# Expert routing of a two-layer mixture kernel: one-hot inversion at the end against lists scattered to DRAM batch by batch

## The reference

```python
x = x + _L0_xattn_ref(ctx_768, _layernorm(x), mask, ...)     # 4 heads; keys: 1024 latents + 77 context rows
x = x + _L0_ffn_ref(_layernorm(x), router_w, w1, b1, w2, b2) # 8 experts, F=1024, relu
x = x + _L1_xattn_ref(_layernorm(x), ctx_768, ...)           # 16 heads, 77 keys
x = x + _L1_ffn_ref(_layernorm(x), gate_w, w1, w2, w3)       # 8 experts, F=512, silu gate
```

```python
logits = x_flat @ router_w.T
probs = softmax(logits); top_w, top_idx = top_k(probs, 2)
top_w = top_w / (sum(top_w) + 1e-9)
out = sum over the two chosen experts of expert(x) * top_w
```

## Time and profile before

| what | value |
|---|---|
| median of 3 runs | 1673.76 us (1672.48 to 1675.39) |
| the profiled execution | 1674.64 us, its span 1672.9 us |
| PE busy | 1475.3 us (88%) |
| DVE busy | 1025.3 us (61%) |
| ACT busy | 837.3 us (50%) |
| POOL busy | 668.4 us (40%) |
| granted TensorE clock, mean | 0.923 of full speed |

### The profile page before, as it was taken

The page is one execution under the profiler, slowest core; times in us unless marked ns, Lnnn a source line. Parts: engine busy times, 40 slices in busy tenths (PEclk is TensorE's granted clock), DMA queues, the critical chain, the costliest instruction groups (busy, mean ns, idle before and its releaser), DMA issues. The chain is left out here.

```text
span 1672.9 us, 36937 instructions
## 1 busy us (share of the span) xinstructions
PE 1475.3 (88%) x12752; PEld 1098.7 (66%) x12752; DVE 1025.3 (61%) x1887; ACT 837.3 (50%) x1583; POOL 668.4 (40%) x495
## 2 busy tenths in 40 slices
PE   6799798898898569999999996999978579999996
PEld 2424334334227559989889984777768469988885
DVE  5666676667667844555554444888858834444543
ACT  2675766766654425556664541667644422222221
POOL 3500402304200015554444443777750036565554
PEclk8899899899895579999999997999985789999998
DMA  5411321313216454567885434100006263355553
GB/s 171 164 51 51 125 75 50 125 50 106 71 51 226 151 213 106 143 163 223 236 233 127 102 65 122 34 25 26 27 1 224 91 205 65 61 138 134 142 133 70
DMA packets 110607, 191.53 MB, mean 114 GB/s; under 512 B 10928, under 2 KB 68580, under 8 KB 110180
## 3 DMA queue, kind: packets, MB, share of 16 engines
q1 hardware_dynamic: 80407, 149.44, 26.6%
q0 software_dynamic: 27264, 37.24, 12.8%
q10 hardware_dynamic: 2791, 2.84, 0.6%
HBM read 122.53 MB, written 66.96 MB: 113 GB/s over the span
## 5 line engine op out<-in xcount | busy, mean ns | idle before, releaser
L1426 PE MATMUL e_ph<-e_zTt,weights_a 128*128 128x256 f16 x2688 | 306.1, 275 | 0.1
L1426 PEld LDWEIGHTS e_ph<-e_zTt,weights_a 128*128 x2688 | 264.9, 99 | 32.7 <-issue 0.4
L1368 POOL DMA_INDIRECT e_zt<-token_parts,slot_token x142 | 146.7, 1033 | 209.7 <-issue 201.7
L1481 ACT ACTIVATE e_h<-e_ph,e_b 128x256 f32<-128x256 f32 (+1 forms) x344 | 128.3, 436 | 154.7 <-PE e_ph L1426 154.3
L1378 POOL DMA_INDIRECT token_rows<-e_ysb,slot_token x71 | 123.2, 1735 | 184.7 <-DVE e_ysb L1554 141.4
L1440 PE MATMUL e_pyt<-weights_b,e_hh 128*128 x1136 | 194.2, 273 | 2.5 <-issue 1.1
L703 ACT ACTIVATE probs<-lower_banks,shift 128x1024 f32<-128x1024 f32 x128 | 137.7, 1112 | 72.9 <-PE lower_banks L577 72.9
L760 DVE TENSOR_TENSOR acc<-acc,probs 128x1024 f32<-128x1024 f32 (+1 forms) x112 | 136.9, 1222 | 52.0 <-ACT probs L703 50.2
L1536 DVE TENSOR_TENSOR e_hl<-e_h,e_hh 128x512 f16<-128x512 f32 x142 | 94.4, 690 | 110.8 <-ACT e_hh L1492 110.6
L1378 POOL DMA_INDIRECT out_dram<-e_ysb,slot_token x71 | 113.1, 1592 | 113.7 <-DVE e_ysb L1557 76.8
L1440 PE MATMUL e_pyt<-weights_b,e_hl 128*128 x568 | 154.8, 273 | 0.0
(11 more groups left out here) (250 smaller groups left out, 2970.8 us busy)
## 6 DMA issues: line engine op xcount, KB each, us to landing
x_sb<-weight_parts SPq DMA_DIRECT2D x30, 1024.0 KB, 7.2
weight_parts<-w_split SPq DMA_DIRECT2D x32, 512.0 KB, 3.3
weights_a<-weight_parts SPq DMA_DIRECT2D x16, 1024.0 KB, 7.4
x_sb<-in_u SPq DMA_DIRECT2D x24, 512.0 KB, 5.3
weight_parts<-x_sb SPq DMA_DIRECT2D x24, 512.0 KB
w_raw<-in_w1T SPq DMA_DIRECT2D x16, 512.0 KB, 4.6
w_raw<-in_w2T SPq DMA_DIRECT2D x16, 512.0 KB, 4.6
weights_b<-weight_parts SPq DMA_DIRECT2D x8, 1024.0 KB, 9.6
```

Of the source, the lines that this page charges most:

```text
L1368: pool.indirect_dma_start(zt[:, i % 2, c, :], None, g.zrows, at).then_inc(ld[i % 2], 16)
L1426: last = pe.matmul(out[:, f, :], weights_up(i, e, wp, k, per[i] * q + f), zTs[:, s, 2 * zp + k, 0:cols[i] * P], start=(n == 0), stop=(n == 5))
L1481: last = act.activation(parted(hidden(h32, n), i)[:, f, :], parted(ph[:, bank_of(i, q)], i)[:, f, :], ACT.Relu, bias=b1[:, bass.ds(e, 1), ...
```

## The change

The one-hot inversion goes. Each expert has a list of CAP = 4096 entries of 8 bytes (token, share) in DRAM. A token's slot is 4096 e + rank, where the rank is counted batch by batch with a running total (`carry`), so the entries of a batch can be written as soon as it is routed: POOL scatters them with one indirect DMA for each tile and choice, 16 for a batch, 64 for a layer. The lists are filled with spare tokens beforehand. When all have landed, ACT loads the entries of the first four tiles (`SOON`) into `slot_tab`, and SP those of the others in `experts`, between its `bring_home` calls; each reads its start from SBUF into a register first. In layer 0, batches 0 to 2 are routed inside steps 4 to 27 of the attention of the following batch (`host`), so `route` has only batch 3 left. AHEAD becomes 3 in layer 0. The loops over batches in `attention0` are written out, and the first half's output moves from step 24 to step 29. The core of the diff:

```diff
+def rank(pe, g, r, b, n, prk):
+    pe.wait_ge(r.tallied, 2 * n - 1)
...
+    pe.matmul(out, g.ones16[:], each(g.carry[:, b:b + 1, :], TB + 1), start=True, stop=False)
+    pe.matmul(out[:, 0:TB, :], g.ones16[:], each(g.base16[:].rearrange("p (o e) -> p o e", o=1), TB), start=False, stop=False)
+    pe.matmul(out[:, 0:TB, :], g.upper16[:], r.wk16[:, t0:t0 + TB, :], start=False, stop=False)
+    for d in range(TB):
+        last = pe.matmul(out[:, d + 1:, :], g.ones16[:], each(r.wk16[:, t0 + d:t0 + d + 1, :], TB - d),
+                         start=False, stop=(d == TB - 1))
...
+def slots(dve, r, b, n, prk):
+    ts = slice(b * TB, (b + 1) * TB)
+    dve.wait_ge(r.rk_done, n)
...
+    step(dve, r, dve.tensor_tensor(r.prod[:], r.oh[:, :, ts, :], ranks, ALU.mult))
+    step(dve, r, dve.tensor_reduce(r.slot[:, :, ts], r.prod[:], AX.X, ALU.add))
+    dve.tensor_copy(r.sloti[:, :, ts], r.slot[:, :, ts]).then_inc(r.slotted, 1)
...
+def scatter(pool, g, r, layer, t):
+    for k in range(2):
+        at = bass.IndirectOffsetOnAxis(ap=r.sloti[:, k, t:t + 1], axis=0)
+        pool.indirect_dma_start(g.lists[layer], at, r.pay[:, t, k, :], None).then_inc(g.scattered[layer], 16)
...
+def bring_table(eng, g, layer, i, tile):
+    n, col, cols = tile
+    s = eng.value_load(g.start[0:1, n:n + 1], min_val=0, max_val=E * CAP)
+    eng.dma_start(g.slot_tab[:, col:col + cols, :].bitcast(I32),
+                  g.lists[layer][bass.ds(s, P * cols), :].rearrange("(p c) w -> p c w", c=cols)
+                  ).then_inc(g.tab_in[layer][tab_group(i)[0]], 16)
```

In `attention0`, on PE, ACT, DVE and POOL (HOST_FROM = 4, HOST_PICK = 21, HOST_RANK = 25; they are called with b - 1, after the step's own work):

```diff
+            def host(b, n):
+                j, odd = divmod(n - HOST_FROM, 2)
+                if not odd and 1 <= j <= TB:
+                    host_logits(b, j - 1)
+                if not odd and 0 <= j < TB:
+                    host_turn(b, j)
+                if n == HOST_RANK:
+                    rank(pe, g, rt, b, b + 1, prkh)
...
+            def host(b, n):
+                j, odd = divmod(n - HOST_FROM, 2)
+                if odd and 0 <= j < TB:
+                    host_copy(b, j)
+                    host_high(b, j)
+                if n == HOST_RANK:
+                    exponents(act, rt, b, b + 1)
...
+            def host(b, n):
+                if n == HOST_PICK:
+                    dve.wait_ge(hlg_done, TB * (b + 1))
+                    read_logits(dve, rt, b, plgh)
+                    pick_top(dve, g, rt, b, b + 1, 0)
...
+                if n == HOST_RANK + 1:
+                    weigh(dve, rt, b, b + 1)
+                if n == HOST_RANK + 2:
+                    slots(dve, rt, b, b + 1, prkh)
...
+                for j in range(TB):
+                    scatter(pool, g, rt, 0, b * TB + j)
```

The end of `route` on ACT, and the start of `experts` on SP and POOL:

```diff
+            act.wait_ge(mapped, 1)
+            act.wait_ge(g.scattered[layer], 32 * T)
+            for i in range(SOON):
+                bring_table(act, g, layer, i, tile_shape(i))
...
-            for e in range(AHEAD, E):
+            upto = SOON
+            for e in range(AHEAD[layer], E):
+                for i in range(upto, min(upto + 2 * TB, NT)):
+                    bring_table(sp, g, layer, i, tile_shape(i))
+                upto = min(upto + 2 * TB, NT)
                 bring_home(sp, g, layer, e)
             if layer == 0:
                 fetch(0)
...
+                group, members = tab_group(i)
+                pool.wait_ge(g.tab_in[layer][group], 16 * members)
```

More of the change, by code:

```diff
@@ L514, in pipeline, with batches @@
                         stage(s - lag)
[L516 to L520, removed]
+        def batches(body):
+            for b in range(B):
+                body(b, b + 1 < B)
         @block.tensor
@@ L883, with tab_group, tile_shape @@
 SINGLES_FROM = 2 * PAIRS - NT
-AHEAD = 5
+CAP = B * S
+TOGETHER = 2
+SOON = 4
+AHEAD = (3, 5)
 AFTER = 2
 LAST = (B - 1) * TB
+def tab_group(i):
+    if i < SOON:
+        return i, 1
+    group = (i - SOON) // TOGETHER
+    return SOON + group, min(TOGETHER, NT - SOON - group * TOGETHER)
+def tile_shape(i):
+    alone = sum(x > SINGLES_FROM and (x - SINGLES_FROM) % 2 == 1 for x in range(i))
+    if i > SINGLES_FROM and (i - SINGLES_FROM) % 2 == 1:
+        return PAIRS + alone, C * PAIRS + alone, 1
+    return i - alone, C * (i - alone), C
 def bring_home(eng, g, layer, e):
@@ L942, in route @@
+        cnti, blocksi, pairsi, oddi = (m.sb(nm(f"ei{i}"), [1, E], I32) for i in range(4))
+        pairs, odd, cum_pairs, cum_odd = (m.sb(nm(f"e{i}"), [1, E]) for i in range(4))
+        ends, leap, apart = (m.sb(nm(f"seg{i}"), [1, SEGMENTS]) for i in range(3))
+        at = m.sb(nm("tile_at"), [1, NT])
+        beyond = m.sb(nm("beyond"), [1, NT, SEGMENTS])
+        begin = m.sb(nm("begin"), [1, NT])
+        owner = m.sb(nm("owner"), [1, NT], I32)
         pz = [m.ps(nm(f"pz{i}"), [P, 4, P]) for i in range(2)]
@@ L976, in _ @@
         def _(pool):
[L977 to L987 removed]
+            number(pool, r)
@@ L988, in _, with turn @@
+            pool.memset(apart[:, E - 1:E], -float((E - 1) * CAP)).then_inc(ready, 1)
+            for b in range(B0, B):
+                pool.wait_ge(r.paid, b - B0 + 1)
+                pool.wait_ge(r.slotted, b - B0 + 1)
+                for t in range(b * TB, (b + 1) * TB):
+                    scatter(pool, g, r, layer, t)
         @block.tensor
         def _(pe):
-            def turn(t):
-                pe.wait_ge(z_done, t + 1)
-                if t >= 2:
-                    pe.wait_ge(ev, t - 1)
+            def turn(l):
+                pe.wait_ge(z_done, l + 1)
+                if l >= 2:
+                    pe.wait_ge(ev, l - 1)
@@ new lines, in _ @@
+            dve.wait_ge(g.stat_roots, RUN - 1)
+            if layer == 0:
+                summarise(dve, g, RUN, EARLY, T, False)
+            for l in range(R):
+                center(l)
+            for l in range(T - FIRST):
+                token_low(l)
+                if l + R < T - FIRST:
+                    dve.wait_ge(lo_done, l + 1)
+                    if FIRST + l + R == EARLY:
+                        dve.wait_ge(g.stat_roots, RUN)
+                    center(l + R)
+                if l == 1 and layer == 1:
+                    summarise(dve, g, RUN, EARLY, T, False)
+                if l >= TB and l % TB == AFTER:
+                    choose(B0 + l // TB - 1)
+                if l >= TB and l % TB == AFTER + 3:
+                    weigh(dve, r, B0 + l // TB - 1, l // TB)
+                    slots(dve, r, B0 + l // TB - 1, l // TB, prk)
```

578 lines of the change are left out of this document (318 added, 260 removed).

## The result

The changed kernel takes 1735.4 us (median of 4 runs, 1731.8 to 1748.4), the kernel before 1674.6 in the same batch: ratio 1.0376, 95% interval 1.0319 to 1.0433. It is slower, by 60.8 us where 39.5 were forecast. The profiled execution took 1731.8 us, with a span of 1730.1, against a span of 1672.9 before.

A forecast was written before the change was run, and what follows sets the result against it. PE was taken to bound attention0, chains of dependent work both routes. Host work +39, route of layer 0 -42.5, experts of layer 0 +22 and route of layer 1 +21 sum to +39.5: 1674.6 becomes 1714 us, range 1660 to 1750.

The forecast's parts named there:

- Host work in attention0: Term: hosted tiles' work on full PE lengthens attention0 by 13 us a batch, three batches, +39 us.
- the sum of 4.64 us: Attention0: loop of PE's step, ACT's copy, cast and exponentials takes 4.64 us for two steps, 4.5 taken, against 3.27.
- Scatters on POOL in attention0: Term: 16 scatters, 20 us, fit a 24 us gap ahead of the next batch's roots, hidden, 4 us to spare.
- Route of layer 0: Term: with only batch 3 left to route, the first gather comes at 556.2 in place of 598.66, -42.5 us.
- Experts of layer 0: Term: SP issues 39 tables and five experts before fetch(0); ACT waits 34.5 us, PE hides 12.5, +22 us, bounds 7.5 and 42.
- Route of layer 1: Term: 64 scatters on POOL move the first gather from 1344.26 to 1365.2, +21 us, bounds +17 and +63.
- POOL is solid with 64 scatters: Sign in layer 1's route: POOL's queue has no gaps, and the first gather comes 109 us after the route's start.
- no stall at tile 2: Rival, experts of layer 0: tables at 0.75 us or less and faster weights keep the fetch hidden; 1692 us, chance 0.20.
- attention absorbs: Rival, attention0: the 4.64 us loop overlaps more than thought and absorbs the host work; 1689 us, chance 0.10.
- cheap scatters: Rival, both routes: POOL's time falls with row size to 0.35 us a scatter; 1660 us, chance 0.15.
- dear ones: Rival, attention0 and both routes: scatters at 1.92 us each, late roots in two batches; 1780 us, chance 0.10.

The follow-up runs named there:

- The cast's move: The changed kernel with the hosted cast to float16 moved from ACT to DVE, after its sum of an odd step: 1728.5 us in one run.
- the tables spread: The changed kernel with fetch(0) and fetch(1) first, then four tables, five bring_homes, and 35 tables two at a time in SP's tile loop: 1703.2 us (1.0156).
- scatters-last run: The changed kernel, but in layer 1's route POOL starts its 64 scatters only when the slots of all four batches are there: 1754.3 us in one run.
- paced run: The changed kernel with a memset of 1024 columns on POOL, waited for, behind every second scatter of layer 1: 1760.6 us in one run.
- ACT's stream shifted: The changed kernel with 24 one-element copies at the start of ACT's part in the route of layer 1: 1737.4 us in one run.

## Why the prediction was right and where not

The direction was right and the time lay in the range, by a sum in which one term was 18 us short, two more were short by 5 and 3.5, and another was 9 us too high. That the last one took back a third of the others is luck; without it the time would have been 1744 us, still inside the range.

*Host work in attention0*, +39 forecast, +30.1 measured. The mechanism held: copies wait for PE's transposes, and two steps with a hosted tile take 4.42 us (212.41 to 216.83) against 4.5 forecast and 3.27 before. Eight of them give 9.2 us, a batch is 10.6 us longer, so the rest (`weight_high` in the loop, last logits, `rank`, late sums) costs 1.4 us by difference and not the 3.2 that I added. The cast's move, worth 0.2 us of its 0.41 for two steps, shows that the loop runs through ACT but not strictly one part after the other, as the sum of 4.64 us had it.

*Scatters on POOL in attention0*, "hidden, with 4 us to spare", held between batches: behind the scatters of the first hosted batch POOL is idle for 4.0 us ahead of the first root (287.93), which waits for DVE. The step that failed is the last batch: behind it no head follows, and the block ends with a wait for the landing. I had named no cover for that end. It costs 3.5 us: the landing ends 0.4 us after the last store, and POOL's drain of 4.0 us stands behind it.

*Route of layer 0*, -42.5 forecast, -41.8 measured; scatters 18.2 us after its start, a cadence of 1.27 us, first gather 47 us after its start. Right in every part, the landing (3.5 us) and the four tables included.

*Experts of layer 0*, +22 forecast, +31.5 measured for the block itself (+26.8 with attention1). The place and the cause were right, and the runs showed both. The term was undersized: a table cost SP 1.18 us (16 in 18.8 us) and not 1.1, ACT's first `weight_high` came 74.4 us after the first gather, 37.0 later than before, and ACT waited 41.0 us, not 34.5; of that PE hid 8 us (41.0 - 33.2), not 12.5. PE's wait stands at tile 4, as forecast, but it ends with DVE's copy of the transposed tokens and not with a bank from ACT: that copy waits in DVE's order behind `e_hl`, and this for ACT (DVE idle for 40.6 us). With the tables spread, 31.7 us come back. A slip of my own in this term: 39 tables at 0.35 us less are 13.7 us, so the lower bound was 8.4 and not 7.5.

*Route of layer 1*, +21 forecast, +39.3 measured, and here the working failed: "POOL is solid with 64 scatters". The first scatter came 22.8 us after the start (20.6 forecast), the cadence was right, and a hole of 15.4 us stood between scatters 32 and 33, which is most of the 18 us. My sum let the tiles of batches 1 to 3 run on beside the scatters as before; the scatters-last run shows them doing so when no scatter runs, and the paced run nearly so at 1.74 us a scatter. Of the path that the sum took, POOL's queue, the price was right; what it lacked is that the scatters delay the work that feeds them.

The rivals: "no stall at tile 2" and "attention absorbs" are refuted by the waits and by the run without hosting; cheap scatters and dear ones both by the median of 0.96 us.

## What to carry to other kernels

When work is moved to a queue, price what stands behind it in that queue customer by customer, and spread cheap, late-needed DMAs between the urgent ones: here the order of 39 small loads on SP cost 32 us, and moving only the first two victims ahead gave back 11. Work put inside a block that ends with a barrier is hidden only if its last completion is early, too, with whatever the engine still runs behind it: here a wait of 0.4 us put a drain of 4.0 us on the path. A gain seen in one execution of one version has to be looked for again in the next: the 7 us of the cast were gone. A producer that streams indirect DMAs beside a fine-grained loop between engines can slow the loop: look for idle stretches whose inputs are ready by the rows.

## What the runs showed of the hardware that was not expected

Back-to-back scatters (128 rows of 8 bytes every 1.27 us) delay the hand-over from PE to ACT. It begins when 8 to 10 of them have been issued and grows to 10 to 12 us (idle stretches of 11 to 13) until they end; it appeared at the same tiles in both layers, with ACT's stream shifted, in runs with and without the other edits, and in attention0 once its scatters started earlier; it vanishes without scatters beside the tiles and nearly at 1.74 us a scatter, and it does not appear in the changed kernel's attention0, where they come 1.47 us apart. Hand-overs from ACT to PE and from ACT to DVE in the same stretch are prompt (1315.97 plus 0.37, then PE at 1316.40). The semaphore's record is late by what ACT waits. Whether PE's work itself or only the signal of its end is late stays open, since the ends of matmuls are modelled in these rows; so does why it takes 8 scatters to begin. A scatter with fewer completions might tell, and was not tried.

POOL's drain at the end of attention0 took 3.98 us in every profiled run that waits there for its scatters, whether the landing had taken 2.1 or 5.3 us; that it does not shrink with an early landing is all that is shown of it.
